# Two heads a slot in bank pairs, q in two f16 parts, and the two score passes issued apart

## The reference

```
xn  = (x - mean) / sqrt(var + 1e-5)
q, k, v = xn @ w.T * s + b          # 16 heads of 8 features
p   = softmax(q @ k.T / sqrt(8))    # per head, 256 x 256
att = (p @ v) @ w_o.T * s_o + b_o
h   = relu(s0 * [xn, -xn] @ K0) * 2  # K are +1 or -1
h   = relu(s1 * h @ K1) * 2          # 512 x 512
out = x + att + s2 * h @ K2
```

## Time and profile before

| | us |
|---|---|
| median of 3 runs | 345.76 (343.56 to 347.13) |
| the profiled execution | 348.12 |
| its span, first to last instruction | 346.3 |
| PE, DVE, ACT, POOL busy | 310.8, 281.3, 237.1, 107.5 |
| mean granted TensorE clock | 0.974 of full speed |

### The profile page before, as it was taken

How to read it: one execution, slowest core, us unless ns; L and a number is a source line. 1 busy time by engine, 2 the same in 40 slices (tenths; PEclk the granted TensorE clock), 3 DMA queues, 4 the chain that set the end, 5 groups by cost and what they waited for, 6 DMA issues and landing times.

```text
span 346.3 us, 9162 instructions
## 1 busy us (share of the span) xinstructions
PE 310.8 (90%) x3248; PEld 174.2 (50%) x3248; DVE 281.3 (81%) x655; ACT 237.1 (68%) x515; POOL 107.5 (31%) x186
## 2 busy tenths in 40 slices
PE   5957789998999999999999998999989999997792
PEld 5734445454554555564555545455645555553331
DVE  4737778888988898888989888988889988988722
ACT  2314286877778696968677785968777786956771
POOL 2332323323242432433232424324222424300000
PEclk9978989999999999999999999999999999999987
DMA  4231314031322313141313223131413223130001
GB/s 122 59 96 40 91 39 112 22 108 38 89 76 64 103 48 102 48 116 35 99 49 85 82 61 103 43 109 42 114 27 100 66 77 88 42 107 4 19 3 31
DMA packets 28415, 23.88 MB, mean 69 GB/s; under 512 B 5698, under 2 KB 25170, under 8 KB 28370
## 3 DMA queue, kind: packets, MB, share of 16 engines
q1 hardware_dynamic: 28370, 23.29, 25.1%
HBM read 15.47 MB, written 7.34 MB: 66 GB/s over the span
## 4 chain that ended last, share of the span: by engine, by line
PE 41%; SPq 26%; DMA 13%; ACT 7%; issue 6%; POOL 3%; DVE 3%; POOLq 0%; ACTq 0%; DVEq 0%
SPq L360 12%; PE st_bank L846 12%; PE ctx_bank L880 10%; DMA q_rows<-max_rows 10%; SPq L365 7%; PE work L938 5%; PE work L908 5%; PE work L894 4%; SPq L352 3%; DMA q_rows<-q_scratch 3%; SPq L392 3%; POOL q_part L325 3%; ACT probs L502 2%; PE work L928 2%; ACT q_part L556 2%
## 5 line engine op out<-in xcount | busy, mean ns | idle before, releaser
L502 ACT ACTIVATE probs<-st_bank 128x512 f32<-128x512 f32 x248 | 148.7, 603 | 67.8 <-PE st_bank L846 64.7
L647 DVE TENSOR_REDUCE neg_max<-s_bank 128x2 f32<-128x512 f32 x248 | 168.5, 683 | 25.3 <-PE s_bank L853 23.0
L846 PE MATMUL st_bank<-q_rows,k_rows 51*128 51x256 bf16 x496 | 94.3, 274 | 15.5 <-DMA q_rows<-max_rows 9.9
L853 PE MATMUL s_bank<-k_rows,q_rows 48*128 48x256 f16 x496 | 95.8, 276 | 3.9 <-DMA q_rows<-q_scratch 3.9
L880 PE MATMUL ctx_bank<-probs,v_ext 128*32 128x256 f32 x1024 | 69.8, 391 | 1.2 <-ACT probs L502 1.2
L846 PEld LDWEIGHTS st_bank<-q_rows,k_rows 51*128 51x128 f16 x496 | 28.9, 94 | 70.7 <-issue 34.3
L901 PE MATMUL work<-r_hi,w 128*128 128x256 f16 x256 | 59.6, 274 | 3.8 <-DVE r_lo L618 2.2
L901 PE MATMUL work<-r_lo,w 128*128 128x256 f16 x256 | 59.2, 272 | 0.0
L722 DVE STREAM_TRANSPOSE turned<-ctx_bank 128x256 f32<-128x256 f32 x64 | 28.6, 446 | 22.3 <-PE ctx_bank L880 21.1
L618 DVE SCALAR_TENSOR_TENSOR r_lo<-work,r_hi 128x512 f16<-128x512 f32 x64 | 43.5, 681 | 3.9 <-ACT r_hi L491 3.8
L491 ACT ACTIVATE r_hi<-work 128x512 f16<-128x512 f32 x64 | 38.3, 602 | 11.4 <-PE work L901 9.8
(11 more groups left out here) (97 smaller groups left out, 393.1 us busy)
## 6 DMA issues: line engine op xcount, KB each, us to landing
k_rows<-k_scratch SPq DMA_DIRECT2D x64, 96.0 KB
q_rows<-q_scratch SPq DMA_DIRECT2D x64, 96.0 KB
q_scratch<-q_part SPq DMA_DIRECT2D x48, 64.0 KB, 2.0
xin<-x SPq DMA_DIRECT2D x16, 128.0 KB, 2.1
k_scratch<-k_part SPq DMA_DIRECT2D x32, 64.0 KB, 2.0
out<-outs SPq DMA_DIRECT2D x16, 128.0 KB, 1.8
q_rows<-max_rows SPq DMA_DIRECT2D x64, 6.0 KB
w_sb<-w SPq DMA_DIRECT2D x1, 256.0 KB, 2.6
```

The lines of the kernel that those rows point to most:

```text
L502: nc.scalar.activation(probs[head // GROUP % 2][:, head % GROUP, :, :].rearrange("p k q -> p (k q)"), exp_banks(s)[t % len(exp_banks(s))][ ...
L647: nc.vector.tensor_reduce(out=neg_max[:, t // HALF, t % 2, t % HALF // 2, :], in_=max_banks(s)[t % len(max_banks(s))][:, :].rearrange("p ( ...
L846: return mm(banks[t % len(banks)][:, kt * SEQ:(kt + 1) * SEQ], k[:, kt * P:(kt + 1) * P], q, start=True, stop=True)
L853: return mm(banks[t % len(banks)][:, qt * SEQ:(qt + 1) * SEQ], q[:, qt * P:(qt + 1) * P], k, start=True, stop=True)
```

## The change

It changes five things at once.

1. **Slots.** A step has 8 slots j with two heads in each. `s_pair` and `st_pair` are two banks wide, one such pair for each pass (while both passes run), so each pass has no second buffer. ACT's exp, DVE's reduce take 128x1024 in one instruction. The context bank's two halves hold two groups, and DVE transposes both at once.
2. **Apart.** `scores_for_max(s, j)` stands at the slot's start and `scores_for_exp(s, j)` about half a slot later, with other work of PE after either of them.
3. **Parts.** q and k are both in two f16 parts: 32 rows, 34 with the maximum in two parts. The scales are computed at the start with one more small matmul, and exp's scale is read from memory (`exp_scale`) instead of being a constant.
4. **Who does it.** DVE copies both high parts in one instruction (128x512), POOL makes both low parts in one. The splitting of the maxima moves from DVE to POOL, three small instructions a half.
5. **DMAs.** Four stores instead of five and four row loads of 128 KB instead of eight of 96 KB. The loads wait until all four stores have landed.

The core of the diff:

```diff
-BANK = {"qk": 0, "l0b": 0, "l1a": 0, "o": 0, "l0a": 1, "l1b": 1, "l2": 1, "xT": 2, "max1": 1, "max0": 2,
-        "v": 2}
+BANK = {"xT": 0, "qk": 0, "l0b": 0, "l1a": 0, "v": 0, "max1": 1, "l0a": 1, "l1b": 1, "l2": 2, "max0": 2, "o": 2}
...
-        def max_banks(s):
-            return s_bank if s.has(2) else s_bank + st_bank
+        def max_pairs(s):
+            return [s_pair] if s.has(2) else [s_pair, st_pair]
...
+            def scores_for_exp(s, j):
+                if j % QUARTER == 0:
+                    s.wait(pe, max_rows_loaded[j // QUARTER], MAX_LOADS, 2, MAX_LOADS)
+                pairs = exp_pairs(s)
+                s.wait(pe, probs_ready, HALF, 2, j if j == 0 else j + 1 - len(pairs))
...
+                for kt in range(TT):
+                    for par in range(2):
+                        q, k = (rows_of(rows, s.third(2), 2 * j + par, MROWS) for rows in (q_rows, k_rows))
+                        c = (TT * par + kt) * SEQ
+                        last = mm(dst[:, c:c + SEQ], k[:, kt * P:(kt + 1) * P], q, start=True, stop=True)
+                last.then_inc(st_psum, 1)
+            def scores_for_max(s, j):
+                if j == 0:
+                    s.wait(pe, rows_loaded, LOADS, 1, LOADS)
+                pairs = max_pairs(s)
+                s.wait(pe, max_ready, HALF, 1, j + 1 - len(pairs))
...
+                    if j == 1 and s.has(0):
+                        s.wait(dve, qk_scaled, 2, 0, 2)
+                        s.wait(dve, hi_stored, 32, 1, 32)
+                        s.wait(dve, lo_ready, 1, 1, 1)
+                        nc.vector.tensor_copy(qk_part[:, 0, :, :], qk[:, :, :]).then_inc(hi_ready, 1)
...
+            USERS = [("xT", 0, xT_copied, 2, 2), ("max1", 2, max_rows_ready, 2, 2), ("qk", 0, qk_scaled, 2, 2),
+                     ("l0a", 0, r0_ready, 2, 1), ("l0b", 0, r0_ready, 2, 2), ("l2", 1, ffn_ready, 1, 1),
+                     ("max0", 1, max_rows_ready, 2, 1), ("l1a", 0, r1_ready, 2, 1), ("l1b", 0, r1_ready, 2, 2),
+                     ("o", 3, out_ready, 1, 1), ("v", 1, v_ready, 1, 1)]
...
+                    s.wait(sp, hi_stored, 32, 0, 32)
+                    s.wait(sp, lo_stored, 32, 0, 32)
+                    s.wait(sp, st_psum, HALF, 3, HALF)
```

More of the change, by code:

```diff
@@ new lines, in step @@
+                    if j == 0 and s.has(0):
+                        s.wait(act, xT_psum, 1, 0, 1)
+                        s.wait(act, v_psum, 1, 2, 1)
+                        s.wait(act, l0_psum, 2, 2, 2)
+                        b = psum("xT")[:, 0:SEQ]
+                        nc.scalar.activation(xT[s.par(0)][:, :], b, ACT.Copy, scale=X_UP).then_inc(xT_copied, 1)
+                        nc.scalar.activation(xT_hi[s.par(0)][:, :], b, ACT.Copy, scale=X_UP).then_inc(xT_copied, 1)
+                    if j == 1 and s.has(2):
+                        copy_max(s, 2, 1)
@@ L507, in step @@
+                    if j == 2 and s.has(0):
+                        s.wait(act, l1_psum, 2, 1, 2)
+                        for k, name in enumerate(("l0a", "l0b")):
+                            s.wait(act, l0_psum, 2, 0, k + 1)
+                            relu_hi(k, psum(name), r0_hi, r0_hi_ready)
+                    if j == 3 and s.has(1):
                         if s.first == 1:
@@ L513, in step @@
                                              ).then_inc(ffn_ready, 1)
-                    for half in range(2):
-                        lag = 1 + half
-                        if t == ACT_SLOT[f"max{half}"] and s.has(lag):
-                            s.wait(act, maxT_psum, 2, lag, half + 1)
-                            s.wait(act, max_rows_loaded[half], MAX_LOADS, lag + 1, MAX_LOADS)
-                            src = psum(f"max{half}")[:, :].bitcast(bf16)
-                            nc.scalar.activation(max_rows[half][:, :], src[0:2 * HROWS, 0:P], ACT.Copy
-                                                 ).then_inc(max_rows_ready, 1)
@@ L578, in step, with copy_max @@
                         ).then_inc(v_ready, 1)
+            def copy_max(s, lag, half):
+                s.wait(act, maxT_psum, 2, lag, half + 1)
+                s.wait(act, max_rows_loaded[half], MAX_LOADS, lag + 1, MAX_LOADS)
+                src = psum(f"max{half}")[:, :].bitcast(f16)
+                nc.scalar.activation(max_rows[half][:, :], src[0:2 * HROWS, 0:P], ACT.Copy
+                                     ).then_inc(max_rows_ready, 1)
             act.wait_ge(half_ready, 2)
@@ new lines, in step @@
+                    if j == 1 and s.first == 0:
+                        split_qk(s, nc.vector, dve)
+                        second_layer_weights(0)
+                    if j == 2 and s.has(0):
+                        s.wait(dve, l1_psum, 2, 1, 2)
+                        for k, name in enumerate(("l0a", "l0b")):
+                            s.wait(dve, r0_hi_ready, 2, 0, k + 1)
+                            relu_lo(k, psum(name), r0_hi, r0_lo, r0_ready)
+                    if j == 2 and s.first == 0:
+                        second_layer_weights(1)
```

584 lines of the change are left out of this document (259 added, 325 removed).

## The result

The changed kernel takes **400.05 us** (median of 4 runs, 394.47 to 406.2), the kernel before 346.44 (343.56 to 348.52) beside it: ratio 1.1405, 95% interval [1.1298, 1.1512]. Executions of one kernel fall into quick and slow ones (here 394.47 and 394.84 us, and 405.27 and 406.2 us), and the ratios in this document compare the quick ones while the medians take in all. I had forecast 367.0 with a range of 339 to 374. The sign was right and the size was not: 14% slower, not 6%. The profiled execution is the one of 405.27 us (span 403.4, mean granted clock 0.895, before 0.974). The one of 394.47 us had a mean clock of 0.923.

A forecast was written before the change was run, and what follows sets the result against it. PE's nearly full work and a chain of waits were taken to bound the kernel. Thirteen step starts gave +25.2 us, the start -3.5 and the end -0.5: +21.2 on the median of 345.76, so 367.0 us, range 339 to 374.

The forecast's parts named there:

- Period: Steady step: 10.9 us up to max 4 plus 10.2 us of PE work, 21.1 us against 19.16.
- The gap before max 4: Mid-step on PE: max 4 waits for DVE's reduce 3, 1.4 us idle.
- at xT: Early in the step: xT shares a bank with v and waits for ACT's copy, PE idle about 0.5 us.
- at l0b: First half of the step: l0b shares bank 0 with qk and waits for ACT's scaling, 0.5 us.
- PE's floor: PE's own work in a step: 18.3 us plus 0.36 for score passes standing apart, 18.7 us.
- the chain: First half of the step: exp 7, v, xT, exp 1, qk, l0b, exp 2, relu, r_lo, reduce 3 cause all three gaps.
- Failed step 1: Second half of the step, max 4 to next max 0: PE's work alone, 10.2 us, reckoned at full clock.
- Failed step 2: Row loads on SP: landed 2.9 to 3.3 us after issue, covered with two microseconds to spare; start 3.5 us shorter.
- Failed step 3: Last steps, 16 to 18: bound by alternation of a pass and its reader, -0.5 us (-2 to +2).
- (a): Steady step: waits are covered and PE is the bound at 18.7 us, 336 us in all; chance 0.21.
- (b): Steady step: wide instructions shorter or work overlaps, a gap of 0.5 to 1 us stays, 346 us; chance 0.12.
- (c): Steady step: slower POOL splits or exp at its upper bound add 0.5 to 0.8 us, 374 to 378 us; chance 0.05.

The follow-up runs named there:

- e5: Changed kernel with exp 2 issued between l0a and l0b, xT in bank 2, and q row loads as four DMAs of 16 rows: 357.82 us.
- e6: As e5, with DVE's reduce 3 ahead of the second r_lo instead of behind it: 351.42 us, ratio 1.0106 to the kernel before.
- e2: Changed kernel with q's row loads as four loads of 16 rows instead of two that repeat 16 rows: 396.42 us.
- e1: Changed kernel with twelve small useless transposes on PE in the idle time before max 4: 390.88 us, ratio 1.1318 to the kernel before.
- e4: Kernel before, with one wait tightened so that PE stands idle before slot 8: 357.82 us, ratio 1.0341.
- e3: Changed kernel with exp 2 issued between l0a and l0b and xT moved to bank 2: 391.5 us, ratio 1.1251 to the kernel before.
- e8: Changed kernel with both the filler transposes of e1 and the split q loads of e2: 382.54 us, ratio 1.0924 to the kernel before.
- g1: Kernel before, its sixteen slots kept, with two f16 parts of q, new scales, exp scale from memory, small stores and split q loads: 580.26 us.
- g2: As g1, with one row of zeros put between, so the passes have 35 and 33 rows: 363.25 us, ratio 1.0338 to the kernel before.
- e7: As e5, with six filler transposes on PE in the gap left before max 4: 358.09 us, ratio 1.0331 to the kernel before.

## Why the prediction was wrong, point by point

**Right: the mechanism of the longer step and its size.** "Period: 10.9 + 10.2 = 21.1 us": undisturbed 20.91. The gap before max 4 was given as 1.4 us (1.47), at xT 0.5 (0.45), at l0b 0.5 (0.21). Exp 1.13 (1.11), reduce 1.18 (1.22), PE's floor 18.7 (18.64 busy in a short step). e5 and e6 confirm the chain by taking its links out: 20.91, 19.48, 19.01. The forecast took from the Trainium skill (Perfetto Trace Analysis, Optimizing Scalar/DVE Operations) that on engines which are not saturated but make bubbles elsewhere, instructions are better broken up. The trace agrees in that DVE's and ACT's busy time of a step fell (17.03 to 15.42 us, 14.64 to 13.73) and the step grew. It does not show that the width did it: e6 has the same wide instructions and a step of 19.01 us.

**Failed step 1: PE at full clock in every step.** The term "the second half, max 4 to the next max 0, is PE's work alone", 10.2 us, was worked out at full clock, as was the whole floor. I put three gaps of 2.4 us together into each step, where the kernel before idles 1.28, and never asked what the clock does with them. It fell in seven of twelve steps of the profiled execution, each time at the end of the gap before max 4 or within 2 us of it: 12 x (22.41 - 20.91) = 18.0 us; in e2's, 6 us. e1, which fills that gap, has no fall in its steps, so the gap is part of their cause; e4 shows that one gap of 1.36 us is not enough for them.

**Failed step 2: the row loads.** "Four loads of 0.74 to 14.8, ... landed at 19.3 to 19.7 (2.9 to 3.3)", and "its rows and maxima should be there at about 39". I took the landing from the earlier trace rows, a load of another shape: 24 rows without a repeat. It was 7.7 us. The landing of the stores, taken as 2.9, was 3.6 to 3.8. This sets the start: +9.1 us where I had -3.5, and e2, by the shape of the load alone, gives 9.4 back. It also makes the second ring that e3 ran into.

**Failed step 3: the end.** "-0.5 (-2 to +2)" was +9.0, of which 1.75 is the thirteenth longer step and 3.0 the fall of the clock in it. The other 4.3 us are not split by an experiment, and their cause stays open; e8, with +11.2, shows that neither the shape of the loads nor the gap before max 4 in the full steps accounts for them.

**The sum.** In us of span of the profiled executions: start 9.1, twelve periods at full clock 12 x 1.75 = 21.0, clock in them 18.0, end 9.0, together 57.1. Of the forecast's +21.2, the period's part, 13 x 1.94 = 25.2 against 13 x 1.75 = 22.8, was right to 10%, and the 36 us beyond the forecast are the three failed steps. The span of the execution of 394.47 us is 392.6, so this sum is 10.8 us smaller there; by its higher mean clock that is an estimate of how much less the clock's terms, 18.0 and 3.0, are in it: about half.

**The rivals.** (a) and (b) did not come. (c) named more waits, with 374 to 378, and missed what they were. None had the clock, and the measured time lies above all of them. And a cost that I did put at nothing, 32 instead of 48 rows, is nothing only because the two passes are apart, as far as g1 and g2 tell.

## What to carry to other kernels

When a change adds a wait to an engine that was nearly full, read the granted clock as a term of the sum: an idle stretch of 1.5 us in PE, in a step with 2.3 us idle, cost its own length and in some steps 1.5 or 3.0 us more for work at half clock. Take a transfer's landing time only from one with the same outermost dimension. And where matmuls of two heights take turns, look whether they start together: here those of 32 and 34 rows did not, and one row of zeros in each was cheap.

## What the runs showed of the hardware

- 64 score matmuls a step with alternating heights of 34 and 32 rows made the kernel 1.67 times as long as the kernel before, and one row more in each took 217 us of it back (g1, g2).
- In g1 the clock also fell where PE was never idle by the profile, so idle time is not the only thing that lowers it. A window of g1:

```profile
180.00:210.00 30.00, 30.00 (x149) 12.86 (x148) 12.54 (x31) 13.52 (x26) 4.58 (x8) 0.61 0.11 32
```

- A load of 128 KB as two copies of 16 rows landed 6.8 to 7.7 us after its issue (changed kernel, e1, e3), the same rows as two loads of 64 KB in 2.1 to 2.2 (e2, e5, e6, e8).
- Useless matmuls in a gap shortened the mean step by 1.4 us against an execution with seven falls of the clock (e1), and did nothing where the clock was not falling (e7).
